# Making the second layer's linear weights in the last batch of the first layer, with the low-rank products on three quarters of the rows

## The chip, the cores and the metric

The kernel runs on one core of a Trainium2 chip. The metric is the device time of one execution in microseconds. Before the change it is 1170.06 us, the median of three runs (1169.66 to 1171.59).

## What is computed

Two transformer layers over x of shape 8 x 512 x 128, each an attention and a feed-forward block side by side on the same normalised input. The first layer has sixteen causal heads and a mixture of 32 experts of which six are taken for each row, with a shared expert. The second has four heads over two key heads, and three blocks of two linear maps each, with their weights in four bits and a low-rank addition:

```
w = q / 7.5 - 1.0                       # 6 matrices of 128 x 128
w = w * repeat(scale, 16, axis=1)
base = einsum('btd,od->bto', x, w) + bias
lora = einsum('btr,or->bto', einsum('btd,rd->btr', x, la), lb)     # r = 32
h = y + h after each block of two, with layernorm and gelu between them
```

The kernel never forms the low-rank term by rows of x. It makes one weight for each of the six maps, `w + (lb la)` transposed, before the second layer begins: the product of the two factors is a matmul over 32 rows of each.

## The kernel before, in words

The work is written out by hand for each engine, with semaphores between the engines. The first layer goes over eight batches of 512 rows. Each batch has two stages on TensorE. First come eight slots, one for each pair of heads: scores, exponentials on ScalarE, transposes of the probabilities, and the weighing of the values, whose result ScalarE copies (L859). Then come seventeen units of the experts (`units`, unit 0 is the shared one). For unit u TensorE does `project_unit(b, u)` (six matmuls of 512 columns), and from unit 3 on `unit_down(b, u - 3)` (three matmuls). Between the two, ScalarE takes the silu (L879), VectorE multiplies by the other half (`gate`, L1293) and by the routing weight of each row (`hidden`, L1303), ScalarE rounds to the high part (L869), and VectorE or POOL makes the low part (L1297, L592). The last units of a batch come down at the head of the next batch (`first_head`), before its slots; its accumulator is copied by ScalarE (L873) in slot 0. In units 5 to 15 of all but the last batch TensorE also does the rows, the router, the queries and keys and the values of the next batch. In batch 7, the last, there is no next batch; units 8, 10 and 12 carry transposes of rows of the second layer (`turn_rows`, into banks 4, 5 and 6) instead.

SP issues the DMAs in one order. In each batch it stores the routing weights (L490), loads them spread over 64 partitions, twice for each unit, into a ring of three buffers `crow` (`spread_weights`, L498, three units ahead), stores the sums of the softmax (L503), and loads these spread for each pair into `rrow` (`spread_sums0`, L510, in units 2, 3, 4, 8, 9, 10, 12, 13). A load into a ring waits until the buffer is free.

The weights of the linear maps are made in batch 0. SP loads the factors `la` and `lb` after pair 0's sums (L528, two DMAs, at unit 2). After unit 16's projection TensorE makes the six products over 32 rows into banks 4 and 5 (`add_lora`, L1550), and ScalarE copies them to `lin` (L776, L777). At the end of batch 0 SP issues ten loads (L533: the four-bit weights and scales into `crow`, the biases into `rrow`) and waits for `lin_ready`. POOL converts them (L620 to L629) and adds them to `lin` (L631) while batch 1 begins. All is needed first by `lin_in` (L1914, L1916), at the end of batch 7.

Of the kernel before, what the change touches and what calls it, by code (L numbers as in the profile page):

```python
# [14 lines left out]
P = 128  # L15
# [8 lines left out]
R, GROUP, NLIN = 32, 16, 6  # L24
BLOCKS = NLIN // 2
# [56 lines left out]
def build(nc, a, out_dram):  # L82
    with ExitStack() as ctx:
# [17 lines left out]
        wqkv_rest = sb("wqkv_rest", [P, 2 * 3 * PAIRS * P - 2 * TILES * TILES * P])  # L101
        with ExitStack() as raw:
            down_raw = raw.enter_context(nc.sbuf_tensor("down_raw", [P, UNITS, D], F32))
# [14 lines left out]
        lin = sb("lin", [P, NLIN, D])  # L118
# [86 lines left out]
        la, lb = (flat_pt[0:R, k * NLIN * D:(k + 1) * NLIN * D].rearrange("p (n d) -> p n d", n=NLIN) for k in (0, 1))  # L205
        lora = lin[:, :, :].rearrange("p i o -> p (i o)")
# [106 lines left out]
        lora_taken = sem("lora_taken")  # L313
# [136 lines left out]
        LORA_AFTER = 16  # L450
# [14 lines left out]
        lora_loads = [(la, a["la"]), (lb, a["lb"])]  # L465
# [5 lines left out]
        def _(sp):  # L471
# [40 lines left out]
            for b in range(B):  # L512
# [6 lines left out]
                for u in range(2, UNITS):  # L519
                    if u + CROWS < UNITS:  # L520
                        spread_weights(b, u + CROWS)
                    if u in SUMS_AFTER:
                        spread_sums0(b, SUMS_AFTER.index(u))
                    if b == 0:
                        sp.wait_ge(y_done, PAIRS)
                        if u == 2:
                            for dst, src in lora_loads:
                                sp.dma_start(dst, src).then_inc(lora_loaded, 16)  # L528
                if b == 0:
                    sp.wait_ge(hm_ready, UNITS - 1)  # L530
                    sp.wait_ge(y_divided, PAIRS)
                    for dst, src in w1_loads:
                        sp.dma_start(dst, src).then_inc(w1_loaded, 16)  # L533
                    sp.wait_ge(lin_ready, 1)
# [10 lines left out]
        def _(pool):  # L545
# [78 lines left out]
            def second_layer_weights():  # L624
# [4 lines left out]
                setup.step(pool.tensor_tensor(wf, wf, qs, ALU.mult))  # L629
                pool.wait_ge(lora_taken, 2)  # L630
                pool.tensor_tensor(lin[:, :, :], lin[:, :, :], wf, ALU.add).then_inc(lin_ready, 1)  # L631
# [24 lines left out]
            for b in range(B):  # L656
# [3 lines left out]
                if b == 0:  # L660
                    second_layer_weights()
                elif b < B - 1:
                    inv_sqrt1(b - 1)
# [80 lines left out]
        def _(act):  # L744
# [26 lines left out]
            def second_layer_weights():  # L771
# [3 lines left out]
                act.wait_ge(lora_done, 1)  # L775
                act.activation(lora[:, 0:512], bank[4], ACT.Copy).then_inc(lora_taken, 1)  # L776
                act.activation(lora[:, 512:NLIN * D], bank[5][:, 0:NLIN * D - 512], ACT.Copy).then_inc(lora_taken, 1)  # L777
# [107 lines left out]
            def first_layer(b):  # L885
                if b:
                    router_exps(b)
                if b == 1:
                    act.activation(temp1[:, 1:2], temp1[:, 0:1], ACT.Exp).then_inc(act_setup, 1)
                    act.wait_ge(lora_taken, 2)  # L890
# [33 lines left out]
                for u in range(UNITS):  # L924
# [12 lines left out]
                    if b < B - 1:  # L937
# [7 lines left out]
                        if b == 0 and u == LORA_AFTER:  # L945
# [152 lines left out]
        def _(dve):  # L1098
# [210 lines left out]

            def first_layer(b):  # L1310
# [22 lines left out]
                for u in range(UNITS):  # L1333
# [15 lines left out]
                    if b < B - 1:  # L1349
                        if u == ROWS_AFTER:  # L1350
                            split_xt(b + 1)
                        if u == LOGITS_AFTER:
                            take_logits(b + 1)
                low_part(b * UNITS + UNITS - 1, UNITS - 1)
# [174 lines left out]
        def _(pe):  # L1529
# [16 lines left out]
            def add_lora():  # L1546
                pe.wait_ge(lora_loaded, 16 * len(lora_loads))
                o = psum[:, 4:6, :].rearrange("p b n -> p (b n)")
                for i in range(NLIN):
                    last = mm(o[:, i * D:(i + 1) * D], la[:, i, :], lb[:, i, :], start=True, stop=True)  # L1550
# [270 lines left out]
            def first_head(b):  # L1821
# [9 lines left out]
                if b == 1:  # L1831
                    pe.wait_ge(lora_taken, 2)
# [8 lines left out]
            def units(b):  # L1841
# [12 lines left out]
                for u in range(2, UNITS):  # L1854
                    project_unit(b, u)
                    if b < B - 1:
# [10 lines left out]
                        if b == 0 and u == LORA_AFTER:  # L1867
                            pe.wait_ge(v_taken, 2 * FILLS)
                            add_lora()
                    elif u in TURN1_AFTER:  # L1870
                        g = TURN1_AFTER.index(u)
                        if g == 1:
                            pe.wait_ge(rinv0_copied, B)
                        if g == 2:
                            pe.wait_ge(y_ready, ROUNDS0)
# [428 lines left out]
```

## Time and profile before

The profiled execution took 1168.83 us, and its span from the first to the last instruction is 1167.0 us.

| | before |
|---|---|
| median of the runs | 1170.06 us |
| the profiled execution | 1168.83 us |
| its span | 1167.0 us |
| TensorE busy | 99% |
| VectorE busy | 85% |
| ScalarE busy | 70% |
| POOL busy | 35% |

Busy time is what the profile shows for each engine; TensorE's matmuls overlap, so its share says that it always has work, not that the array is full. A timeline row is the start in us, the duration, the engine, the line of the code, the operation, its tiles, the shapes and the count of instructions that were merged; in brackets stands the idle time before it and what ended that. PE is TensorE's matmuls, PEld its weight loads, DVE is VectorE, ACT ScalarE, SPq the queue of SP's DMA issues.

### The profile page before, as it was taken

How to read it: one execution, taken by the hardware profiler on the slowest of the kernel's cores; microseconds unless marked ns; L12 is line 12 of the kernel's file. 1: busy time of each engine (PE TensorE's matmuls, PEld its weight loads, DVE VectorE, ACT ScalarE, POOL GpSimd, SP SyncE). 2: the span in 40 equal slices, each digit the busy share in tenths (PEclk: the TensorE clock that was granted, in tenths of full speed). 3: DMA queues.
4: the chain of work that ended last, by engine and by line, in shares of the span. 5: the costliest groups of instructions: out<-in, count | busy, mean ns of one | idle time of the engine just before them, and what ended most of it. 6: DMA issues, size and time to landing. Idle time of an engine off the chain costs nothing.

```text
span 1167.0 us, 23979 instructions
## 1 busy us (share of the span) xinstructions
PE 1150.2 (99%) x8932; PEld 889.8 (76%) x8932; DVE 986.9 (85%) x1918; ACT 811.7 (70%) x2184; POOL 408.1 (35%) x365
## 2 busy tenths in 40 slices
PE   8999999999999999999999999999999999999998
PEld 6778778777776877677777777777778767777776
DVE  7988698979887989788888988898888778898897
ACT  6885677567756775677557765776577767877886
POOL 2326610730064006400550055005500577735741
PEclk9999999999999999999999999999999999999999
DMA  8014300410131003100320032003300330000001
GB/s 267 2 31 145 94 1 31 136 55 2 31 128 64 1 25 131 66 2 20 112 90 2 11 115 97 1 6 117 99 2 3 124 96 1 1 20 19 1 11 29
DMA packets 44565, 63.93 MB, mean 55 GB/s; under 512 B 8160, under 2 KB 18656, under 8 KB 44192
## 3 DMA queue, kind: packets, MB, share of 16 engines
q1 hardware_dynamic: 44448, 62.39, 16.6%
q8 instruction: 71, 1.16, 0.4%
q14 instruction: 46, 0.38, 0.1%
HBM read 59.48 MB, written 2.88 MB: 53 GB/s over the span
## 4 chain that ended last, share of the span: by engine, by line
PE 87%; DVE 6%; ACT 2%; issue 2%; POOL 1%; DMA 1%; SPq 0%; DVEq 0%; ACTq 0%; POOLq 0%
PE psum L1647 15%; PE psum L1666 13%; PE psum L1588 11%; PE psum L64 10%; PE psum L66 10%; PE psum L65 10%; PE psum L1703 5%; PE psum L1601 2%; PE psum L1613 2%; PE psum L1916 2%; PE psum L1670 1%; PE psum L1535 1%; PE psum L1972 1%; ACT probs L835 1%; DVE mneg L1247 1%
## 5 line engine op out<-in xcount | busy, mean ns | idle before, releaser
L793 ACT ACTIVATE probs<-psum,mneg 128x256 f32<-128x256 f32 (+3 forms) x400 | 187.3, 486 | 112.2 <-DVE mneg L1228 111.9
L1647 PE MATMUL psum<-ident,probs 128*128 128x128 f32 x1600 | 210.3, 276 | 3.6 <-ACT probs L835 3.4
L1228 DVE TENSOR_REDUCE mneg<-psum 128x2 f32<-128x1024 f32 (+3 forms) x256 | 194.1, 819 | 15.3 <-PE psum L1601 11.3
L1647 PEld LDWEIGHTS psum<-ident,probs 128*128 128x128 f32 x1600 | 178.0, 141 | 30.6 <-ACT probs L793 8.2
L1219 DVE COPY pt<-psum 128x512 f32<-128x512 f32 x256 | 164.9, 683 | 38.7 <-PE psum L1647 36.9
L592 POOL TENSOR_TENSOR qk_lo<-sg,qk_hi 128x512 fp32r<-128x512 f32 x64 | 91.7, 1438 | 155.5 <-ACT qk_hi L869 155.5
L1666 PE MATMUL psum<-pt,v_all 128*64 128x384 f32 (+5 forms) x1088 | 142.6, 412 | 0.0
L556 POOL TENSOR_TENSOR rstd<-var,mhalf 128x4 f32<-128x4 f32 x7 | 7.1, 1012 | 385.6 <-DVE var L1112 385.6
L1666 PEld LDWEIGHTS psum<-pt,v_all 128*64 128x64 f32 (+1 forms) x1088 | 69.7, 135 | 62.7 <-issue 50.2
L64 PE MATMUL psum<-xt_hi,gu_hi 128*128 128x512 f32 x272 | 110.2, 405 | 0.0
L66 PE MATMUL psum<-xt_hi,gu_lo 128*128 128x512 f32 x272 | 107.7, 396 | 0.0
L588 POOL TENSOR_TENSOR yt<-yt,rrow 128x512 f32<-128x512 f32 x64 | 98.9, 1551 | 24.5 <-DMA rrow<-sums 24.4
L65 PE MATMUL psum<-xt_lo,gu_hi 128*128 128x512 f32 x272 | 107.3, 394 | 0.0
L1303 DVE TENSOR_TENSOR sg<-sg,crow 128x512 f32<-128x512 f32 x88 | 98.3, 1117 | 7.8 <-DMA crow<-weights 5.0
L879 ACT ACTIVATE sg<-psum 128x512 f32<-128x512 f32 x96 | 57.0, 595 | 48.7 <-PE psum L66 48.6
L1588 PE MATMUL psum<-qk_hi 64*128 64x256 f32 (+3 forms) x512 | 88.5, 342 | 0.2 <-DVE v_all L1288 0.2
L1208 DVE SCALAR_TENSOR_TENSOR qk_lo<-psum,qk_hi 128x512 fp32r<-128x512 f32 x72 | 49.7, 690 | 44.5 <-ACT qk_hi L816 44.4
L793 ACT ACTIVATION_READ_ACCUMULATOR probs<-psum,mneg 128x1 f32 x400 | 83.6, 209 | 0.0
L1588 PE MATMUL psum<-qk_hi,qk_lo 64*128 64x256 f32 (+3 forms) x512 | 82.3, 318 | 0.0
L1588 PE MATMUL psum<-qk_lo,qk_hi 64*128 64x256 f32 (+3 forms) x512 | 82.3, 318 | 0.0
L869 ACT ACTIVATE qk_hi<-sg 128x512 fp32r<-128x512 f32 x96 | 60.3, 628 | 28.3 <-DVE sg L1303 28.1
L1293 DVE TENSOR_TENSOR sg<-sg,psum 128x512 f32<-128x512 f32 x96 | 65.2, 680 | 17.3 <-ACT sg L879 17.0
(294 smaller groups left out, 2762.3 us busy)
## 6 DMA issues: line engine op xcount, KB each, us to landing
crow<-weights SPq DMA_DIRECT2D x256, 128.0 KB, 2.9
rrow<-sums SPq DMA_DIRECT2D x128, 128.0 KB, 3.0
gu_raw<-in_gu SPq DMA_DIRECT2D x1, 2176.0 KB, 12.4
x_all<-in_x SPq DMA_DIRECT2D x8, 256.0 KB, 5.5
out_rows<-x_all SPq DMA_DIRECT2D x7, 256.0 KB, 2.3
down_raw<-in_down SPq DMA_DIRECT2D x1, 1088.0 KB, 13.0
wqkv_raw<-in_wqkv SPq DMA_DIRECT2D x1, 768.0 KB, 6.1
wqkv_raw<-in_wqkv SPq DMA_DIRECT2D x1, 512.0 KB, 5.1
```

What stands on the lines that cost most here:

```text
L64: nc.tensor.matmul(out, lh, rh, start=start, stop=False, **kw)
L65: nc.tensor.matmul(out, lh, rl, start=False, stop=False, **kw)
L66: return nc.tensor.matmul(out, ll, rh, start=False, stop=stop, **kw)
L588: pool.tensor_tensor(yt[:, p, :], yt[:, p, :], rrow[:, n % RROWS, :], ALU.mult).then_inc(y_divided, 1)
L592: pool.tensor_tensor(hm_lo[u % 3], sg[u % 3], hm_hi[u % 3].bitcast(F32), ALU.subtract).then_inc(pool_lo_ready, 1)
L793: last = act.activation(probs[:, h * HALF + PROB[t]:h * HALF + PROB[t] + w], bank[score_bank(rnd, c) + h][:, o:o + w], ACT.Exp, bias=mneg[ ...
L1219: dve.tensor_copy(pt[:, s % 2, :, 3 - s // 2, :], turn_bank(rnd, s).rearrange("p (j q) -> p j q", q=P)).then_inc(pt_ready, 1)
L1228: last = dve.tensor_reduce(mneg_h[:, :, t], psum[:, b:b + 2, o:o + P * (t + 1)], AX, ALU.max, negate=True)
L1303: dve.tensor_tensor(sg[u % 3], sg[u % 3], crow[:, m % CROWS, :], ALU.mult).then_inc(hm_ready, 1)
L1588: ins = mm(bank[score_bank(rnd, c) + h][:, o:o + w], ql[r, 0, qs_], kl[r, 1, ks], start=i == 0 and n == 0 and not masked, stop=masked, **K)
L1647: last = nc.tensor.transpose(dst[:, i * P:(i + 1) * P], probs[:, v:v + P], ident[:, :])
L1666: last = mm(Y[c:c + m, first * P:T], v(k), rows_t[:, k, first:TILES, :].rearrange("p t q -> p (t q)"), start=(k == 0), stop=(k == TILES - ...
```

## The change

All of the making of the weights moves to the end of the first layer, and the low-rank products take another form.

- `lin` has no memory of its own any more. It lies where the low part of the first layer's value weights was, which are read last in batch 6, for batch 7's values.
- The base weights: SP issues the ten loads at the end of batch 6 and waits there for `wf_ready` instead of `lin_ready` at the end of batch 0. POOL converts after batch 6's units, waits that the last values are made, and writes the product with the scales straight into `lin`.
- The factors: six loads instead of two. Matrix j * 3 + k goes to the k-th quarter of 32 partitions, at place j. They are issued by SP in batch 7 at the same place as before in batch 0, after pair 0's sums.
- The products: TensorE makes them in batch 7 after unit 6's projection, with the three quarters one after the other for each j, into banks 4, 5 and 6.
- The addition: VectorE adds the products to `lin` after its part of unit 6. ScalarE's two copies and POOL's addition are gone.
- Waits: `lora_taken` is gone. The waits for `rinv0_copied` and `y_ready` go from the row transposes of units 10 and 12 to `add_lora`; the transposes of unit 8 wait for `lin_ready`.

```diff
+LORA_TILES = 3
+        lin = wqkv_rest[:, PAIRS * P:PAIRS * P + NLIN * D].rearrange("p (i o) -> p i o", o=D)
-        lin = sb("lin", [P, NLIN, D])
-        la, lb = (flat_pt[0:R, k * NLIN * D:(k + 1) * NLIN * D].rearrange("p (n d) -> p n d", n=NLIN) for k in (0, 1))
-        lora = lin[:, :, :].rearrange("p i o -> p (i o)")
+        la, lb = (pt1[0:LORA_TILES * R, 0, 0, 2 * k:2 * k + 2, :] for k in (0, 1))
-        LORA_AFTER = 16
+        LORA_AFTER, W1_AFTER = 6, 16
-        lora_loads = [(la, a["la"]), (lb, a["lb"])]
+        lora_loads = [(v[r * R:(r + 1) * R, :, :], a[n].rearrange("r (j k) d -> k r j d", k=LORA_TILES)[r, :, :, :])
+                      for v, n in ((la, "la"), (lb, "lb")) for r in range(LORA_TILES)]
...
@@ SP
-                    if b == 0:
-                        sp.wait_ge(y_done, PAIRS)
-                        if u == 2:
-                            for dst, src in lora_loads:
-                                sp.dma_start(dst, src).then_inc(lora_loaded, 16)
-                if b == 0:
-                    sp.wait_ge(hm_ready, UNITS - 1)
-                    sp.wait_ge(y_divided, PAIRS)
+                    if b == B - 1 and u == 2:
+                        sp.wait_ge(y_done, ROUNDS0)
+                        for dst, src in lora_loads:
+                            sp.dma_start(dst, src).then_inc(lora_loaded, 16)
+                if b == B - 2:
+                    sp.wait_ge(hm_ready, (B - 1) * (UNITS - 1))
+                    sp.wait_ge(y_divided, (B - 1) * PAIRS)
                     for dst, src in w1_loads:
                         sp.dma_start(dst, src).then_inc(w1_loaded, 16)
-                    sp.wait_ge(lin_ready, 1)
+                    sp.wait_ge(wf_ready, 1)
@@ POOL
-                setup.step(pool.tensor_tensor(wf, wf, qs, ALU.mult))
-                pool.wait_ge(lora_taken, 2)
-                pool.tensor_tensor(lin[:, :, :], lin[:, :, :], wf, ALU.add).then_inc(lin_ready, 1)
+                pool.wait_ge(v_done, B * FILLS)
+                pool.tensor_tensor(lin, wf, qs, ALU.mult).then_inc(wf_ready, 1)
...
-                if b == 0:
+                if 0 < b < B - 1:
+                    inv_sqrt1(b - 1)
+                if b == B - 2:
                     second_layer_weights()
-                elif b < B - 1:
-                    inv_sqrt1(b - 1)
@@ ScalarE
-                act.wait_ge(lora_done, 1)
-                act.activation(lora[:, 0:512], bank[4], ACT.Copy).then_inc(lora_taken, 1)
-                act.activation(lora[:, 512:NLIN * D], bank[5][:, 0:NLIN * D - 512], ACT.Copy).then_inc(lora_taken, 1)
...
-                    act.wait_ge(lora_taken, 2)
@@ VectorE
+            def add_lora():
+                dve.wait_ge(wf_ready, 1)
+                dve.wait_ge(lora_done, 1)
+                tiles = lin.rearrange("p (j k) d -> p k j d", k=LORA_TILES)
+                products = psum[:, 4:4 + LORA_TILES, 0:2 * D].rearrange("p k (j d) -> p k j d", d=D)
+                dve.tensor_tensor(tiles, tiles, products, ALU.add).then_inc(lin_ready, 1)
...
+                    elif u == LORA_AFTER:
+                        add_lora()
@@ TensorE
                 pe.wait_ge(lora_loaded, 16 * len(lora_loads))
-                o = psum[:, 4:6, :].rearrange("p b n -> p (b n)")
-                for i in range(NLIN):
-                    last = mm(o[:, i * D:(i + 1) * D], la[:, i, :], lb[:, i, :], start=True, stop=True)
+                pe.wait_ge(rinv0_copied, B)
+                pe.wait_ge(y_ready, ROUNDS0)
+                for j in range(NLIN // LORA_TILES):
+                    for i in range(LORA_TILES):
+                        r = slice(i * R, (i + 1) * R)
+                        last = mm(bank[4 + i][:, j * D:(j + 1) * D], la[r, j, :], lb[r, j, :], start=True, stop=True)
...
-                if b == 1:
-                    pe.wait_ge(lora_taken, 2)
...
-                        if b == 0 and u == LORA_AFTER:
-                            pe.wait_ge(v_taken, 2 * FILLS)
-                            add_lora()
+                    elif u == LORA_AFTER:
+                        add_lora()
                     elif u in TURN1_AFTER:
                         g = TURN1_AFTER.index(u)
-                        if g == 1:
-                            pe.wait_ge(rinv0_copied, B)
-                        if g == 2:
-                            pe.wait_ge(y_ready, ROUNDS0)
+                        if g == 0:
+                            pe.wait_ge(lin_ready, 1)
                         turn_rows(0, g, 4)
```

## Rows read from the trace of the kernel before

**Rows 1.** The page: busy time and share, granted clock by slices, chain by engine.

```profile
PE 1150.2 (99%) x8932; PEld 889.8 (76%) x8932; DVE 986.9 (85%) x1918; ACT 811.7 (70%) x2184; POOL 408.1 (35%) x365
PEclk9999999999999999999999999999999999999999
PE 87%; DVE 6%; ACT 2%; issue 2%; POOL 1%; DMA 1%; SPq 0%; DVEq 0%; ACTq 0%; POOLq 0%
```

**Rows 2.** Timeline of ScalarE: last Y copy of batches 0 to 2, next accumulator copy.

```profile
87.97 0.60 ACT L859 ACTIVATE yt<-psum 128x512 f32<-128x512 f32 x1 [0.73 <-PE psum L1670]
...
142.90 0.60 ACT L873 ACTIVATE rrow<-psum 128x512 f32<-128x512 f32 x1 [0.22 <-PE psum L1703]
...
207.20 0.60 ACT L859 ACTIVATE yt<-psum 128x512 f32<-128x512 f32 x1 [1.20 <-PE psum L1670]
...
260.40 0.60 ACT L873 ACTIVATE rrow<-psum 128x512 f32<-128x512 f32 x1 [0.22 <-PE psum L1703]
...
324.70 0.60 ACT L859 ACTIVATE yt<-psum 128x512 f32<-128x512 f32 x1 [1.20 <-PE psum L1670]
...
378.41 0.60 ACT L873 ACTIVATE rrow<-psum 128x512 f32<-128x512 f32 x1 [0.22 <-PE psum L1703]
```

**Rows 3.** Timeline of TensorE around the low-rank products, batch 0.

```profile
126.11 0.40 PE L66 MATMUL psum<-xt_hi,gu_lo 128*128 128x512 f32 x1
...
126.43 1.60 PE L1550 MATMUL psum<-pt 32*128 32x128 f32 x12
...
127.96 0.50 PE L64 MATMUL psum<-qk_hi,down_hi 128*128 128x512 f32 x1
```

**Rows 4.** Timeline of SP's queue: the two loads of the factors, batch 0.

```profile
95.13 0.58 SPq L528 DMA_DIRECT2D pt<-in_la  x1
95.75 0.42 SPq L528 DMA_DIRECT2D pt<-in_lb  x1
```

**Rows 5.** Timeline of SP's queue, batch 7: the store, then units 1 to 5.

```profile
902.10 0.33 SPq L490 DMA_DIRECT2D weights<-comb  x1
...
914.98 4.54 SPq L498 DMA_DIRECT2D crow<-weights  x4
919.56 1.23 SPq L510 DMA_DIRECT2D rrow<-sums  x2
920.84 1.24 SPq L498 DMA_DIRECT2D crow<-weights  x2
922.13 1.23 SPq L510 DMA_DIRECT2D rrow<-sums  x2
```

**Rows 6.** First Y copies of batches 1 and 2 on ScalarE; POOL's addition, by its line.

```profile
151.58 0.62 ACT L859 ACTIVATE yt<-psum 128x512 f32<-128x512 f32 x1
...
269.09 0.63 ACT L859 ACTIVATE yt<-psum 128x512 f32<-128x512 f32 x1
...
L631 POOL TENSOR_TENSOR lin<-lin,crow x1: 1825/1825/1825, 147.6 to 147.6; 128x768 f32<-128x768 f32 x1
```

**Rows 7.** DMA issues: engine, count, KB each, median us from issue to landing.

```profile
crow<-in_qs SPq DMA_DIRECT2D x8, 48.0 KB, 2.6
...
pt<-in_la SPq DMA_DIRECT2D x1, 96.0 KB, 2.9
```

**Rows 8.** Timeline of TensorE, batch 7: the first matmul after unit 6's projection.

```profile
923.10 0.40 PE L64 MATMUL psum<-qk_hi,down_hi 128*128 128x512 f32 x1
```

**Rows 9.** Timeline of TensorE: score products, two heads on 64 rows each.

```profile
136.21 0.39 PE L1588 MATMUL psum<-qk_lo,qk_hi 64*128 64x512 f32 x2
...
136.44 0.39 PE L1588 MATMUL psum<-qk_hi,qk_lo 64*128 64x512 f32 x2
```

**Rows 10.** Timeline of VectorE, batch 7: hidden of unit 5, gate of unit 6.

```profile
922.49 0.69 DVE L1303 TENSOR_TENSOR probs<-probs,crow 128x512 f32<-128x512 f32 x1 [0.23 <-DMA crow<-weights]
...
924.12 0.69 DVE L1293 TENSOR_TENSOR sg<-sg,psum 128x512 f32<-128x512 f32 x1 [0.94 <-ACT sg L879]
```

**Rows 11.** Timeline of TensorE, batch 7: its waits for low parts after unit 6.

```profile
935.14 0.50 PE L64 MATMUL psum<-hm_third,down_hi 128*128 128x512 f32 x1 [0.52 <-DVE hm_third L1297]
...
942.50 0.50 PE L64 MATMUL psum<-hm_third,down_hi 128*128 128x512 f32 x1 [0.36 <-POOL hm_third L592]
```

More of the change, by code:

```diff
@@ L312, in build @@
         lora_done = sem("lora_done")
-        lora_taken = sem("lora_taken")
+        wf_ready = sem("wf_ready")
         lin_ready = sem("lin_ready")
@@ L944, in first_layer @@
                             take_values(b + 1, range(2 * (u - V_AFTER), 2 * (u - V_AFTER) + 2))
-                        if b == 0 and u == LORA_AFTER:
+                        if b == 0 and u == W1_AFTER:
                             second_layer_weights()
@@ L1866, in units @@
                             project_values(b + 1, range(2 * (u - V_AFTER), 2 * (u - V_AFTER) + 2))
-                        if b == 0 and u == LORA_AFTER:
-                            pe.wait_ge(v_taken, 2 * FILLS)
-                            add_lora()
+                    elif u == LORA_AFTER:
+                        add_lora()
                     elif u in TURN1_AFTER:
                         g = TURN1_AFTER.index(u)
-                        if g == 1:
-                            pe.wait_ge(rinv0_copied, B)
-                        if g == 2:
-                            pe.wait_ge(y_ready, ROUNDS0)
+                        if g == 0:
+                            pe.wait_ge(lin_ready, 1)
                         turn_rows(0, g, 4)
```

## Prediction

> **What bounds the kernel now.** I read the page first. TensorE is busy for 99% of the span, nearly all of the chain that ended last is its matmuls, and its clock stands at the upper of the two levels (2.4 GHz) in all forty slices [rows 1]. So time is lost or won only where TensorE's own queue gets longer or shorter, or where it stands still. The second view is the timeline of ScalarE at two fixed points of each batch: the copy of the last pair's Y in the unit stage (L859) and the copy of the accumulator in the next batch (L873). From the one to the other takes 142.90 - 87.97 = 54.93 us in batch 0, 53.20 us in batch 1 and 53.71 us in batch 2 [rows 2]; the later batches repeat one or the other value. Batch 0 is thus 1.2 to 1.7 us longer than its sisters, and what it alone has is the low-rank products. The third view is the timeline of all engines in the two places that the change touches, the end of batch 0's units and units 2 to 9 of batch 7.
>
> **Out of batch 0: the products.** After unit 16's last matmul at 126.11 stand twelve passes of L1550 (two for each of six fp32 products), and `unit_down` begins at 127.96 [rows 3]. From one matmul of 512 columns to the next it is 0.23 us, so the insertion takes 127.96 - 126.11 - 0.23 = 1.62 us of a TensorE that waits for nothing else. Nothing is late behind it. The low part that `unit_down(14)` wants is made long before, and the accumulator's copy follows TensorE by 0.22 us of idle [rows 2], so it moves forward with it. ScalarE also loses its two copies of the products, which were beside TensorE's work: nothing. SP loses two issues at 95.13 and 95.75 [rows 4], but TensorE doesn't stand still in these units: nothing. Gain: 1.62 us; the distance between batches bounds it at 1.2 and 1.7.
>
> **From batch 0 to batch 6: the base weights.** Ten issues on SP, SP's wait for `wf_ready`, and POOL's conversion move from the start of batch 1's attention to that of batch 7's. SP's next task there is to store the routing weights, at 902.10 in batch 7 [rows 5], some 50 us after; nothing queues behind its wait. The same POOL work lies in batch 1 now: from the accumulator's copy to the next Y copy it is 151.58 - 142.90 = 8.68 us there, and 269.09 - 260.40 = 8.69 us in batch 2 without it [rows 2, 6]. So it slows TensorE's slots not at all, and I take nothing for it in batch 7 either. POOL loses the addition of 1.83 us [rows 6], off the path. Its new wait, for the value projections of batch 7, is met before it is reached, since those are made in batch 6's units 12 to 15.
>
> **Into batch 7: six loads on SP.** They stand after unit 5's weights and pair 0's sums, that is behind 919.56 + 1.23 = 920.79, where SP now goes straight on to unit 6's weights at 920.84 and pair 1's sums at 922.13 [rows 5]. SP has no free time in this stretch. An issue of 96 KB over 32 partitions took 0.58 us behind a 64-row one and 0.42 behind its own kind [rows 4]; two issues of 64 rows take 1.23 us, 0.62 each [rows 5]. The new ones have 32 partitions with two pieces of 512 bytes each and 32 KB; no row shows this form. Bounds: 0.62 + 5 x 0.47 = 2.97 us for all, and 6 x 0.64 = 3.8 us. I take 3.1, near the 32-partition row. The last issue then starts at about 923.5 (923.3 to 924.1). From issue to landing the 96 KB loads took 2.9 us, the 48 KB ones 2.6 [rows 7]; for 32 KB I take 2.7, with 2.2 to 3.1 as bounds (2.2 is 0.4 below the median of the 48 KB loads). So the factors are there at 926.2 (925.5 to 927.2).
>
> The Trainium skill speaks against this cut: "DMA: Bandwidth & Descriptors", section "Measured (HBM→SBUF, 128 partitions, SWDGE, issued from GpSimd)", says that transfers under 64 KB are ruled by their descriptors and wants loads batched. The rows agree that half the bytes hardly save time [rows 7]. The page's fixed cost of about 2.0 us (section "Anatomy of one DMA — SWDGE (gpsimd) path") would give, as an estimate, a landing some 0.6 us sooner and a sum smaller by that; the rows of this kernel are longer, and I go by them.
>
> **Into batch 7: TensorE waits for them.** `add_lora` stands after unit 6's projection, in front of `unit_down(3)`, which starts at 923.10 today [rows 8]. TensorE's queue is in order, so it stands from 923.10 to 926.2: 3.1 us (2.4 to 4.1). Behind it wait `unit_down(3)`, unit 7's projection and all that hangs on that. Its two other new waits (`rinv0_copied`, `y_ready`) are met: SP's own issues at 914.98 come after the first, and the Y copy stands at ScalarE's unit 1.
>
> **Into batch 7: the products on row quarters.** Twelve passes again. In batch 0 they took 1.53 us one after another [rows 3]. What quarters of the rows do is not in the trace; what halves do is: two products on 64 rows each, 512 columns, begin together and the next two 0.23 us later [rows 9], the distance of one. So disjoint rows do run together. With all three quarters side by side it is 0.5 us, with none 1.6 us; the two passes of one product lie on the same rows and are next to each other in the queue, so I take half of the saving: 0.9 us.
>
> The Trainium skill, "TensorEngine Tiling (Array Packing)", section "Key Properties", says that tiles load weights and multiply in parallel, but that a change of the tiling mode drains the engine. By the first the price would be 0.5 us, by the second a little is added at either end. The halves in this trace agree with the first.
>
> **What of it is taken back.** TensorE is late by 3.1 + 0.9 = 4.0 us, the other engines only by SP's 3.1 us, because unit 6's weights land that much later: VectorE waits for its weights in unit 5 already today (0.23 us) and starts unit 6's gate at 924.12 [rows 10]. TensorE has two waits for low parts later in this stage, 0.52 and 0.36 us [rows 11]; as it arrives 0.9 us later against the others, about the first of them goes. The addition on VectorE (768 elements; 0.69 us for 512 with a PSUM operand [rows 10], so about 1.0 us) is done while TensorE does `unit_down(3)` and unit 7; it may delay gate 7 by up to 0.5 us and is what keeps the second wait alive. Batch 7: 4.0 - 0.5 = +3.5 us (2.7 to 4.5).
>
> **Sum.** -1.62 + 3.5 = +1.9 us. The profiled execution took 1168.83 us for a span of 1167.0; the change is the same on it and on the median of 1170.06, so the forecast is 1170.06 + 1.9, about 1171.9 us.
>
> **Rivals.**
> (a) Forecast, TensorE stands about 3 us for the last load: 1171.0 to 1173.2. Chance 0.60.
> (b) Slower side: SP's queue. If each new issue takes 0.62 us or more and lands after 3.1 us, the last lands at 927.2, TensorE is late by 5.0 us and the weights of units 6 and 7 by 3.8, and little is absorbed: +4.5 - 1.6 = +2.9 us, 1173.0; with 0.8 us an issue +3.9, 1174.0. It decides from 0.58 us an issue upwards. For it: pairs of 64-row issues show 0.62 [rows 5]. Against it: 0.42 at 32 partitions [rows 4]. Chance 0.17.
> (c) Slower side: the clock. The stand of 3 us is longer than any wait of TensorE in the stages around, where the clock never fell [rows 1]. If it fell, matmuls at half rate would be 0.47 instead of 0.23 us apart, 2.1 us more for each unit of nine: +4.0, 1174.0 for one unit. Chance 0.08. The Trainium skill, "TensorE: Matmul & The Clock Gate", section "HAM oscillation — how this bites in real kernels", describes such a fall after waits for a DMA. No row here shows one.
> (d) Nothing stands: the factors land before 923.10, or the later units' waits swallow the stand. Then only the products are left: -1.62 + 0.9 = -0.7, 1169.4; with both later waits gone (0.88) 1168.5. Against it: even at 0.42 us an issue the last one can't start before 923.2. Chance 0.12.
> (e) It does not do what it says: the quarters run one after another, +0.6 on (a), 1172.5; inside the range of (a).
> What is left, 0.03, is a gain of over 2.3 us by something that the trace does not show.
>
> **How the numbers follow.** 0.2% of 1170 is 2.3 us, about what a measurement of this kernel can tell from no change. Of (a), a fifth lies above 1172.4 (0.12); with nearly all of (b) and (c), 0.32 for slower. The rest of (a), (d) and a little of (b) give 0.65 for the same, and 0.03 for faster. The range goes from 1169.4 (the upper form of (d)) to 1174.2 (the upper forms of (b) and (c)).
>
> **What would show it right or wrong.** In the profile of the changed kernel: batch 0's distance between the two copies falls from 54.93 to 53.2 to 53.7 us; SP shows six issues of 0.42 to 0.6 us between 919 and 923 (all times 1.6 earlier); TensorE has one wait of about 3 us in front of L1550's matmuls, ended by a DMA; these span 0.5 to 1.6 us; batch 7's L859 to its end grows by 3 to 4 us; batch 7's first slots keep their 8.69 us. Wrong would be: no wait at L1550, a landing under 2.2 us, a lower clock after the stand, or a longer slot at the head of batch 7.

## The result, and the profile after

The changed kernel takes 1172.58 us, the median of 13 runs (1170.86 to 1173.57). The kernel before, run beside it, takes 1169.66 us (13 runs, 1167.24 to 1171.59). The ratio is 1.0026, with an interval of 1.0018 to 1.0033: about 3 us slower. The ratio is just past the bound of 0.2% that the prediction names, and the lower end of its interval just short of it. The profiled executions are 1172.82 and 1168.83 us, with spans of 1171.0 and 1167.0, so 4.0 us lie between the two that are read here.

The same two points on ScalarE as in [rows 2], now L855 and L869, first for batch 0, then for batch 7. Timeline of the changed kernel; the bracket is the idle time before and what ended it:

```profile
87.97 0.60 ACT L855 ACTIVATE yt<-psum 128x512 f32<-128x512 f32 x1 [0.73 <-PE psum L1678]
...
141.16 0.60 ACT L869 ACTIVATE rrow<-psum 128x512 f32<-128x512 f32 x1 [0.22 <-PE psum L1711]
...
911.75 0.60 ACT L855 ACTIVATE yt<-psum 128x512 f32<-128x512 f32 x1 [1.20 <-PE psum L1678]
...
965.09 0.61 ACT L869 ACTIVATE rrow<-psum 128x512 f32<-128x512 f32 x1
```

The kernel before, batch 7:

```profile
913.70 0.60 ACT L859 ACTIVATE yt<-psum 128x512 f32<-128x512 f32 x1 [1.20 <-PE psum L1670]
...
961.00 0.62 ACT L873 ACTIVATE rrow<-psum 128x512 f32<-128x512 f32 x1
```

Batch 0's distance is 141.16 - 87.97 = 53.19 us, 1.74 less than in [rows 2]. From there to the last Y copy of batch 7 another 0.2 us are scattered over the other batches, whose distances move by up to 0.5 us in either direction: 911.75 against 913.70, so 1.95 us are gained by then. Batch 7's distance goes from 47.30 to 53.34 us, **6.04 us more**. What follows, the second layer, is the same to 0.1 us. So the answer lies in batch 7 alone, and there three engines are to be read.

SP's queue in the changed kernel, where [rows 5] stood before:

```profile
918.90 1.94 SPq L528 DMA_DIRECT2D pt<-in_la  x3
920.88 1.87 SPq L528 DMA_DIRECT2D pt<-in_lb  x3
922.79 1.23 SPq L499 DMA_DIRECT2D crow<-weights  x2
```

The loads of the factors by their line, same kernel (one line for each kind: count, ns of an issue, first and last start), and their time from issue to landing:

```profile
L528 SPq DMA_DIRECT2D pt<-in_la x3: 594/595/669, 918.9 to 920.2; - x3
L528 SPq DMA_DIRECT2D pt<-in_lb x3: 593/593/594, 920.9 to 922.2; - x3
...
DMA to landing us min/median/max: 2.0/2.2/2.6
```

The six issues fill SP from 918.90 to 922.79, 3.9 us, and unit 6's weights come after them. They were the next thing in line before [rows 5].

TensorE in the changed kernel, from the end of unit 6's projection on, where [rows 8] stood:

```profile
920.91 0.40 PE L67 MATMUL psum<-xt_hi,gu_lo 128*128 128x512 f32 x1
924.32 0.79 PE L1558 MATMUL psum<-pt 32*128 32x128 f32 x12 [3.00 <-DMA pt<-in_lb]
925.04 0.80 PE L65 MATMUL psum<-qk_hi,down_hi 128*128 128x512 f32 x1
...
926.06 0.63 PE L67 MATMUL psum<-qk_hi,down_lo 128*128 128x512 f32 x1
926.49 0.63 PE L65 MATMUL psum<-xt_hi,gu_hi 128*128 128x512 f32 x1
...
928.69 0.40 PE L65 MATMUL psum<-qk_hi,down_hi 128*128 128x512 f32 x1
...
943.61 0.51 PE L65 MATMUL psum<-qk_hi,down_hi 128*128 128x512 f32 x1 [0.75 <-DVE qk_lo L1292]
...
955.23 0.50 PE L65 MATMUL psum<-qk_hi,down_hi 128*128 128x512 f32 x1 [0.63 <-DVE qk_lo L1292]
```

The clock beside it, from the table by stretches (start and end, length, then busy time and count for PE, PEld, DVE, ACT and POOL, then the granted clock as a part of the upper level, DMA share, GB/s):

```profile
922.00:924.00 2.00, 0.00 (x0) 0.00 (x0) 1.07 (x2) 1.02 (x2) 0.88 (x1) 1.00 0.19 49
924.00:926.00 2.00, 1.69 (x14) 1.36 (x15) 0.00 (x0) 0.00 (x0) 1.61 (x2) 0.71 0.57 166
926.00:928.00 2.00, 2.00 (x6) 1.55 (x5) 1.51 (x2) 0.00 (x0) 0.00 (x0) 0.50 0.62 203
928.00:930.00 2.00, 2.00 (x9) 1.59 (x9) 0.53 (x2) 1.11 (x3) 0.00 (x0) 0.94 0.63 213
```

VectorE, changed kernel:

```profile
926.49 0.69 DVE L1298 TENSOR_TENSOR sg<-sg,crow 128x512 f32<-128x512 f32 x1 [3.38 <-DMA crow<-weights]
927.10 0.95 DVE L1311 TENSOR_TENSOR wqkv_rest<-wqkv_rest,psum 128x768 f32<-128x768 f32 x1
```

Two instructions of POOL and VectorE in the same kernel, just before TensorE's wait at 943.61, and the same two in the run of "TensorE kept busy in the stand" below:

```profile
941.72 1.29 POOL L588 TENSOR_TENSOR yt<-yt,rrow 128x512 f32<-128x512 f32 x1 [0.44 <-DMA rrow<-sums]
941.75 1.80 DVE L1292 TENSOR_TENSOR qk_lo<-sg,qk_hi 128x512 fp32r<-128x512 f32 x1
```

```profile
941.02 0.68 DVE L1293 TENSOR_TENSOR qk_lo<-sg,qk_hi 128x512 fp32r<-128x512 f32 x1
941.10 1.76 POOL L589 TENSOR_TENSOR yt<-yt,rrow 128x512 f32<-128x512 f32 x1 [0.55 <-DMA rrow<-sums]
```

Taken against the last Y copy, TensorE reaches `unit_down(3)` at 13.29 us instead of 9.40, so **3.89 us late**: 924.32 - 920.91 - 0.23 = 3.18 of standing, and 0.72 for the products. The clock is still at the upper level through the stand (1.00 in the first line). It then falls to the lower one (1.2 GHz, the 0.50 in the third line), and for some three microseconds the matmuls are 0.43 us apart instead of 0.23. `unit_down(4)` begins at 16.94 instead of 11.49: **1.56 us** more. The last 0.59 us are two things. By the row transposes of unit 12 TensorE has won back 0.66 us (28.42 us behind the Y copy against 23.63, so 4.79 late instead of 5.45), mostly because the first wait of [rows 11] is gone. Then it loses 1.25 us at two waits for low parts, 0.75 and 0.63 us. The first of these low parts took VectorE 1.80 us instead of 0.68: it began 0.03 us behind an addition of POOL's, and in the other run 0.08 us ahead of it. The sum is 3.89 + 1.56 + 0.59 = 6.04. Meanwhile VectorE too is late: it stands 3.38 us for unit 6's weights.

### The profile page after: what moved, and what is told of

Same layout as the page of the kernel before. It is cut to its first block, busy times and chain, and to the rows that moved or that the text cites. A ratio compares the mean times of both kernels' runs of the same rounds, so it can differ in the third digit from the quotient of the medians.

```text
span 1171.0 us, 23968 instructions
## 1 busy us (share of the span) xinstructions
PE 1150.5 (98%) x8932; PEld 890.2 (76%) x8932; DVE 991.9 (85%) x1919; ACT 810.3 (69%) x2182; POOL 403.1 (34%) x364
## 4 chain that ended last, share of the span: by engine, by line
PE 84%; DVE 9%; ACT 3%; issue 2%; DMA 1%; SPq 1%; POOL 0%; DVEq 0%; ACTq 0%; POOLq 0%
PE psum L1655 14%; PE psum L1674 13%; PE psum L1596 11%; PE psum L65 10%; PE psum L67 9%; PE psum L66 9%; PE psum L1711 5%; PE psum L1609 2%; PE psum L1621 2%; PE psum L1919 2%; DVE probs L1298 1%; PE psum L1678 1%; DVE sg L1298 1%; PE psum L1540 1%; PE psum L1975 1%
## 5 line engine op out<-in xcount | busy, mean ns | idle before, releaser
L1298 DVE TENSOR_TENSOR sg<-sg,crow 128x512 f32<-128x512 f32 x88 | 102.8, 1168 | 9.1 <-DMA crow<-weights 6.3
```

Of the source, the lines that this page charges most:

```text
L1298: dve.tensor_tensor(sg[u % 3], sg[u % 3], crow[:, m % CROWS, :], ALU.mult).then_inc(hm_ready, 1)
```

## The experiments

From this one profile two explanations fit. Either TensorE's stand and the clock that falls after it are the loss, and VectorE's wait is covered by it; or SP's 3.9 us in front of every later weight load is the loss, and TensorE would have had to wait for VectorE anyhow. Each expectation says what the two give. The measure that is used throughout is batch 7's distance, from the last Y copy to the accumulator's copy: 47.30 us before, 53.34 after. It is read from one execution of each version. In the middle batches, where nothing was changed, this distance moves between 53.19 and 53.79 us, so differences of half a microsecond say nothing.

### The loads where SP has nothing to do

Between the weights of the first three units and the store of the sums SP issues nothing for some seven microseconds. The six loads go there, each still of 32 KB:

```diff
+                if b == B - 1:
+                    sp.wait_ge(y_done, ROUNDS0 - 4)
+                    for dst, src in lora_loads:
+                        sp.dma_start(dst, src).then_inc(lora_loaded, 16)
                 store_sums(b)
...
-                    if b == B - 1 and u == 2:
-                        sp.wait_ge(y_done, ROUNDS0)
-                        for dst, src in lora_loads:
-                            sp.dma_start(dst, src).then_inc(lora_loaded, 16)
```

> The changed kernel with its six loads of the factors moved forward on SP, from behind unit 5's weights to in front of the store of the softmax sums, where SP stands idle for about 6 us. Theory A (TensorE stands because the loads are issued late, and the fall of the clock and SP's delay follow from that): no wait of TensorE in front of the products, clock 1.000 in every execution, unit 6's weights as early as in the kernel before; batch 7 grows only by the products, 0.7 us, against 1.7 us saved in batch 0: about 1.0 us under the kernel before (ratio 0.9991). Theory B (the cost lies in the products, in VectorE's addition or in the moved base weights): the time stays near the changed kernel's, 3 us above before (ratio 1.0026).

It takes 1166.98 us (11 runs) against 1169.4 for the kernel before (27 runs): ratio 0.9984, interval 0.9975 to 0.9993. It is 1.9 us faster than the kernel before and about 5 us faster than the changed one. SP's queue, then TensorE and ScalarE, in this version:

```profile
906.29 2.59 SPq L520 DMA_DIRECT2D pt<-in_la  x3
908.93 1.87 SPq L520 DMA_DIRECT2D pt<-in_lb  x3
913.35 0.49 SPq L504 DMA_DIRECT2D sums<-rl  x1
```

```profile
922.06 0.72 PE L1558 MATMUL psum<-pt 32*128 32x128 f32 x12
...
941.53 0.50 PE L65 MATMUL psum<-hm_third,down_hi 128*128 128x512 f32 x1 [0.46 <-POOL hm_third L592]
```

```profile
912.57 0.60 ACT L855 ACTIVATE yt<-psum 128x512 f32<-128x512 f32 x1 [1.20 <-PE psum L1678]
...
960.00 0.61 ACT L869 ACTIVATE rrow<-psum 128x512 f32<-128x512 f32 x1
```

The last load is issued before 911, and SP still stands until the store at 913.35. The products have no bracket any more: nothing is waited for. Batch 7's distance is 47.43 us, 0.13 more than before; the 0.72 us of the products are nearly all taken back, most of it since the first of the two later waits of [rows 11] is gone. So the whole loss in batch 7 comes from where the loads were issued. This run doesn't say through which of the two ways, since it removes both. The clock isn't at 1.000 in every execution, as was expected, but below it in 2 of 11.

### TensorE kept busy in the stand

Fourteen products of the identity are put in front of the wait, into bank 4, which the real products overwrite:

```diff
+                pe.wait_ge(rinv0_copied, B)
+                for _ in range(KEEP):
+                    mm(bank[4][:, 0:P], ident[:, :], ident[:, :], start=True, stop=True)
                 pe.wait_ge(lora_loaded, 16 * len(lora_loads))
```

> The changed kernel, with 14 products of the identity with itself on TensorE in front of its wait for the factors (their results are overwritten). TensorE works instead of standing; the loads land no sooner. Theory A (the clock falls because TensorE stands, and that costs 1.5 us of its own): clock 1.000 in all executions, the distance from unit 6's projection to unit 3's down stays at about 3.9 us, and the time is 1.4 us under the changed kernel, +1.5 us against before (ratio 1.0013). Theory B (the slower matmuls behind the stand cost nothing, since other engines are late there anyway): the same time as the changed kernel, ratio 1.0026.

It takes 1171.0 us (11 runs), ratio 1.0016 (1.0007 to 1.0025). TensorE and ScalarE:

```profile
925.10 0.72 PE L1562 MATMUL psum<-pt 32*128 32x128 f32 x12
...
944.61 0.50 PE L66 MATMUL psum<-hm_third,down_hi 128*128 128x512 f32 x1 [0.39 <-POOL hm_third L593]
```

```profile
912.50 0.60 ACT L856 ACTIVATE yt<-psum 128x512 f32<-128x512 f32 x1 [1.20 <-PE psum L1682]
...
963.11 0.61 ACT L870 ACTIVATE rrow<-psum 128x512 f32<-128x512 f32 x1
```

The products come as late as in the changed kernel (12.60 us behind the Y copy against 12.57), so SP's part and the length of the gap are untouched; the clock is at the upper level in 9 of 11 executions. Batch 7's distance is 50.61 us, 2.73 under the changed kernel's, and by the ratios (1.0026 and 1.0016) the two differ by about 1.2 us. Of the 2.73 us, 1.48 are there by the transposes of unit 8 (19.04 and 17.56 us behind the Y copy). The other 1.25 us are the long low part and the waits behind it, which this run doesn't have. They are not the clock's: the run with two loads below has both waits (0.73 and 0.49 us) in an execution whose clock never fell in this stage. So the fall of the clock is worth 1.2 to 1.6 us, and with it healed 50.61 - 47.30 = 3.3 us of loss are left.

### The products one unit later

```diff
-        LORA_AFTER, W1_AFTER = 6, 16
+        LORA_AFTER, W1_AFTER = 7, 16
```

> The changed kernel with the products after unit 7's projection instead of unit 6's, 2.1 us of work later. SP's six issues stay where they are. Theory A (the stand is the whole of the cost): the stand shrinks from 3.2 to about 1.1 us, the clock stays up, and the time is 3.5 us under the changed kernel's: -0.6 us against before (ratio 0.9995). Theory B (SP's delay of unit 6's and 7's weights by 3.9 us costs as much by itself, through the gates and low parts that come late): the time is only 1 to 2 us under the changed kernel's, ratio 1.0010 to 1.0018, with waits of TensorE for low parts in units 9 to 12.

It takes 1175.13 us (5 runs), ratio 1.005 (1.0037 to 1.0062): slower still. Batch 7's distance is 967.62 - 913.29 = 54.33 us. TensorE, and under it VectorE:

```profile
925.80 0.72 PE L1558 MATMUL psum<-pt 32*128 32x128 f32 x12 [0.86 <-DMA pt<-in_lb]
...
932.43 0.66 PE L1540 MATMUL psum<-ident,v_all 128*128 128x128 f32 x4 [3.62 <-DVE wqkv_rest L1311]
```

```profile
928.02 0.69 DVE L1298 TENSOR_TENSOR sg<-sg,crow 128x512 f32<-128x512 f32 x1 [3.35 <-DMA crow<-weights]
930.82 0.69 DVE L1298 TENSOR_TENSOR sg<-sg,crow 128x512 f32<-128x512 f32 x1 [1.50 <-DMA crow<-weights]
931.43 0.95 DVE L1311 TENSOR_TENSOR wqkv_rest<-wqkv_rest,psum 128x768 f32<-128x768 f32 x1
```

The stand for the factors shrinks from 3.18 to 0.86 us, as it should. But unit 8's transposes wait for the addition (`lin_ready`), the addition stands behind two products with routing weights on VectorE, and these wait for late loads, 3.35 and 1.50 us. TensorE stands 3.62 us there instead, and the clock falls after that (0.50 from 934 to 936, and below 1 as a mean in all 5 executions). The stand was moved, not removed.

To take that coupling out, the addition was put in front of VectorE's routing product, all else as in the last one:

```diff
+                    if b == B - 1 and u == LORA_AFTER:
+                        add_lora()
                     if u:
...
-                    elif u == LORA_AFTER:
-                        add_lora()
```

> The changed kernel with the products after unit 7, and VectorE's addition in front of its hidden part of unit 7 instead of behind it. In the run with the addition behind, it waited for unit 7's late weights, and TensorE stood 3.6 us for the sum in front of the transposes of unit 8. Theory A (that order was the whole of the surprise): the 3.6 us are gone, the stand for the factors stays at 0.9, the clock stays up, distance in batch 7 48.5 to 50 us instead of 54.3, ratio about 0.9995 to 1.0005. Theory B (SP's delay costs by itself): 51 us or more with waits of TensorE for low parts, ratio 1.0015.

It takes 1171.51 us (11 runs), ratio 1.0013 (1.0004 to 1.0022). TensorE:

```profile
924.33 0.72 PE L1558 MATMUL psum<-pt 32*128 32x128 f32 x12 [0.81 <-DMA pt<-in_lb]
...
928.82 0.66 PE L1540 MATMUL psum<-ident,v_all 128*128 128x128 f32 x4 [1.47 <-DVE wqkv_rest L1311]
...
938.90 0.50 PE L65 MATMUL psum<-xt_hi,gu_hi 128*128 128x512 f32 x1 [0.92 <-DVE sg L1288]
```

No stand is over 1.5 us and the clock stays up in 8 of 11 executions, the profiled one among them, yet batch 7's distance is 52.40 us. The single large wait has become a row of small ones (1.47, 0.82, 0.92 and 0.48 us; two are not shown), the last ended by POOL and the others by VectorE. By the ratios half of the changed kernel's loss is gone, 1.5 of 3.0 us.

### SP's delay alone, and the stand alone

Both start from the version with the early loads. In the first the same six loads are issued a second time at their old place, into memory that nothing reads:

```diff
-                        for dst, src in lora_loads:
-                            sp.dma_start(dst, src).then_inc(lora_loaded, 16)
+                        for dst, src in again_loads:
+                            sp.dma_start(dst, src).then_inc(again_loaded, 16)
...
```

> The kernel with the factors loaded early, and in the changed kernel's place behind pair 0's sums the same six loads once more, into memory that nobody reads. SP is thus late by 3.9 us as in the changed kernel, but TensorE finds its factors and doesn't stand. Distance in batch 7 from the last Y copy to the accumulator copy: 47.4 us with the loads early, 53.3 in the changed kernel. Theory A (TensorE's stand is the cost, SP's delay is taken up by the three units between a projection and its down): 47.5 to 49 us, ratio about 0.999. Theory B (SP's delay of unit 6's and 7's weights is enough by itself: hidden, high and low part come 3 to 4 us late, and TensorE then waits in unit 9 instead): 50 to 51.5 us, ratio about 1.0010.

In the second SP is left alone and TensorE waits ahead of the products for unit 6's `hidden`, which has nothing to do with them:

```diff
                 pe.wait_ge(lora_loaded, 16 * len(lora_loads))
+                pe.wait_ge(hm_ready, (B - 1) * (UNITS - 1) + LORA_AFTER)
```

> The kernel with the factors loaded early, but TensorE waits in front of the products until VectorE has made unit 6's hidden part. TensorE stands for about 3 us at the same place as in the changed kernel, and SP is not late. Theory A (the stand and the clock are the cost): distance in batch 7 47.4 + 3.1 + 1.5, some 52 us, clock 0.997 to 0.998 in most executions, ratio 1.0022. Theory B (a stand is taken up if SP's weights are on time): 49 us or less, ratio 0.9995.

SP's delay alone: 1170.95 us (11 runs), ratio 1.0010 (1.0001 to 1.0019). Batch 7's distance is 51.41 us, 3.98 over the 47.43 of the early loads. Its TensorE (the bracket is the largest of its four waits, the others are 0.25, 0.63 and 0.48 us):

```profile
919.66 0.72 PE L1565 MATMUL psum<-pt 32*128 32x128 f32 x12
...
926.53 0.66 PE L1547 MATMUL psum<-ident,v_all 128*128 128x128 f32 x4 [1.75 <-DVE wqkv_rest L1318]
```

and its VectorE:

```profile
924.92 0.69 DVE L1305 TENSOR_TENSOR sg<-sg,crow 128x512 f32<-128x512 f32 x1 [3.39 <-DMA crow<-weights]
```

By unit 8's transposes TensorE is 1.91 us later than with the early loads (16.36 us behind the Y copy against 14.45). That half of the 3.98 us comes by the addition, which stands on VectorE behind the late product, and by the wait for `lin_ready` that the change put in front of these transposes. How much SP's delay would cost without that coupling wasn't run.

The stand alone: 1173.34 us (8 runs), ratio 1.0029 (1.0019 to 1.004). Its distance is 964.64 - 912.15 = 52.49 us, 5.06 over the early loads, and its TensorE has one line:

```profile
925.44 0.72 PE L1559 MATMUL psum<-pt 32*128 32x128 f32 x12 [3.72 <-issue]
```

The clock is below 1 in all 8 executions. TensorE comes to the products 3.80 us later than with the early loads (13.29 us behind the Y copy against 9.49), and by unit 8's transposes it is 5.35 us late: 1.55 us are what the lower level costs. In the rest of the stage 0.3 us are won back; no later wait of TensorE is left. A stand of this length without the fall of the clock, and without SP's delay, wasn't run.

So **both explanations are right, each by itself**. The delay of SP costs 4.0 us with no stand at the products, the stand with its fall of the clock 5.1 with no delay, and both together 53.34 - 47.43 = 5.9 us, far from their sum of 9.0. The ratios, set against that of the early loads (0.9984), give 3.0 us for the delay, 5.3 for the stand and 4.9 for both; the stand made here was also 0.7 us longer than the changed kernel's. Both make the same units late by the same few microseconds, one along VectorE and one along TensorE, and the later of the two counts. The run with TensorE kept busy bears this out: it has SP's delay and products just as late, but no fall of the clock, and takes 1171.0 us, where SP's delay alone takes 1170.95. On top of either comes the clock. That is why taking away only one of them brings back half at most (unit 7 with the addition first) or nothing (unit 7).

### Two loads instead of six

The factors lie in memory by quarters, so that one DMA over 96 partitions fills all three:

```diff
-        lora_loads = [(v[r * R:(r + 1) * R, :, :], a[n].rearrange("r (j k) d -> k r j d", k=LORA_TILES)[r, :, :, :])
-                      for v, n in ((la, "la"), (lb, "lb")) for r in range(LORA_TILES)]
+        lora_loads = [(la, a["la"]), (lb, a["lb"])]
```

> The changed kernel with the factors laid out by quarters in memory, so that two loads of 96 partitions do what six of 32 did, at the same place in SP's queue. Theory A (the price is the count of issues, 0.64 us each): SP is late by 1.3 us instead of 3.9, the last load lands 2.6 us sooner, TensorE stands for about 0.6 us, the clock stays up; -0.3 us against before (ratio 0.9997). Theory B (the price is the number of pieces or the bytes, not the issues): the two issues take 1.9 us each, and nothing changes against the changed kernel (ratio 1.0026).

It takes 1169.69 us (11 runs), ratio 1.0004 (0.9994 to 1.0013). SP and TensorE:

```profile
919.27 0.58 SPq L527 DMA_DIRECT2D pt<-in_la  x1
919.89 0.43 SPq L527 DMA_DIRECT2D pt<-in_lb  x1
920.37 1.09 SPq L498 DMA_DIRECT2D crow<-weights  x2
```

```profile
923.08 0.72 PE L1557 MATMUL psum<-pt 32*128 32x128 f32 x12 [1.39 <-DMA pt<-in_lb]
```

SP's delay is 1.1 us instead of 3.9, for the same bytes. The stand is 1.4 us, more than was expected, because the larger load takes about 3 us from its issue where the small ones took 2.2. The clock is below 1 in 5 of 11 executions. This is the measured price of the cut into six: 2.6 us by the ratios (1.0026 and 1.0004 of 1170 us), and 3.2 by batch 7's distances (53.34 and 50.14). It lies in the number of issues: the bytes are the same, and an issue of 96 KB in 96 pieces took no longer (0.43 to 0.58 us) than one of 32 KB in 64 pieces (0.59 to 0.67). The fall of the clock is part of this price, as the profiled execution with two loads has none behind its stand of 1.4 us.

### The base weights alone

The kernel before, with only the base weights moved to the end of batch 6:

```diff
-                if b == 0:
-                    sp.wait_ge(hm_ready, UNITS - 1)
-                    sp.wait_ge(y_divided, PAIRS)
+                if b == B - 2:
+                    sp.wait_ge(hm_ready, (B - 1) * (UNITS - 1))
+                    sp.wait_ge(y_divided, (B - 1) * PAIRS)
                     for dst, src in w1_loads:
...
```

POOL's conversion and addition, left out here, move with them.

> The kernel before with nothing but the base weights moved: SP's ten loads and its wait, and POOL's conversion with its addition, go from the end of batch 0 to the end of batch 6. The low-rank products stay in batch 0. Theory A (this part is free): ratio 1.0000 within the interval, and the head of batch 7 (accumulator copy to first Y copy) stays at 8.7 us. Theory B (POOL's or SP's work disturbs batch 7): batch 7 longer by a microsecond or more, ratio 1.001.

It takes 1169.65 us (11 runs) against 1169.72 (30 runs), ratio 1.0000 (0.9991 to 1.0008). The head of batch 7, from the accumulator's copy to the first Y copy, is 858.71 - 850.03 = 8.68 us, as everywhere (8.67 to 8.71), and the distance in batch 7 is 47.45 us. This part is free.

## Why the prediction was right or wrong

It said 1171.9 us, 1169.4 to 1174.2, with most of the chance on no difference. The time is 1172.58, inside; but the ratio is past 0.2%, on the side that was given 0.32. That the time lies near the forecast is in part luck: of the signs that the prediction itself named as showing it wrong, a lower clock after the stand came true, and the shortest landings (2.0 us) were under its 2.2. Point by point:

- **Products out of batch 0.** Said -1.62 with 1.7 as the upper bound; the distance fell by 1.74, a hair more. Right. That nothing was late behind them holds: the idle time of 0.22 us in front of the accumulator's copy is the same.
- **Base weights.** Said free; the run of that part alone shows 1.0000, and batch 7's head is unchanged. Right.
- **SP's six issues.** Said 3.1 us in all (2.97 to 3.8), from the row of 0.42; they took 3.9, at 0.59 to 0.67 each, past the upper end. This term was mis-sized. Reading the row of the second load in [rows 4] as the price of its kind was the error: in the run with two loads it is 0.43 again, where each partition's data lie in one piece as in [rows 4]. Three loads of strided pieces are nearer to the 64-row ones of [rows 5]; that the pieces are the reason isn't shown.
- **Landing.** Said 2.7 us (2.2 to 3.1); the median is 2.2. The page of the Trainium skill that was weighed there, "DMA: Bandwidth & Descriptors", section "Anatomy of one DMA — SWDGE (gpsimd) path", gives its fixed part of about 2.0 us for DMAs that GpSimd issues. These are SP's, and it was still nearer to them (2.0 to 2.6) than the rows of larger loads. Slower issues and a quicker landing cancelled out in the stand: 3.1 said, 3.18 by the starts.
- **Products on quarters.** Said 0.9 (0.5 to 1.6); 0.72 in every version, against 1.53 for the same twelve passes in [rows 3]. With 0.5 for all three side by side, that is four fifths of the saving and not the half. The rule of the Trainium skill, "TensorEngine Tiling (Array Packing)", section "Key Properties", that tiles multiply in parallel, agrees with 0.72; of its drain at a change of mode these rows show at most the 0.2 us over the estimate of 0.5.
- **TensorE late.** Said 4.0 us; 3.89 at `unit_down(3)`. Right, with the two errors above cancelling.
- **The clock, rival (c).** Said 0.08, because no stretch of the kernel before had a lower level, and left out of the sum; the granted clock is below 1 in 12 of 13 executions, and the one at 1.000 is the fastest of them all (1170.86 us). This is the step that failed. "No row here shows one" was no evidence, for no row had a stand of 3 us either: the largest in the stage was 0.52 [rows 11]. And [rows 1] could hardly have shown such a fall, as a slice there is 29 us long: the changed kernel's page has a 9 in all forty slices too. The price was less than the rival's 2.1 us a unit: 1.56, since the clock rose again after some three microseconds. The Trainium skill, "TensorE: Matmul & The Clock Gate", section "HAM oscillation — how this bites in real kernels", describes just this, a wait for a DMA and then work at the lower level. The trace agrees, but for the start: the products right behind the stand still took their 0.72 us. It deserved more than 0.08.
- **What is taken back.** Said 0.5 us, as TensorE would arrive later than the others. By unit 12's transposes it was 0.66 us here, and 0.68 to 0.80 in the runs with the early loads, with TensorE kept busy, with the stand alone and with two loads. So the reasoning held. What the sum didn't have are the 1.25 us that were lost behind it, when a low part on VectorE took 1.80 us in place of 0.68; the run with two loads lost 1.19 us in the same way, the other three nothing. In the kernel before, the timeline has 36 low parts of VectorE (L1297) in rows by themselves: 11 take 1.77 or 1.78 us and all begin while POOL adds `yt` and `rrow`, and 25 take 0.68 us and none of them does. Whether the two meet here hangs on tenths of a microsecond, so this part of the result is luck too. It is read from the traces; no run was made to test it. The wait of 0.75 us ends with that low part, while the second one, 0.63 us, is put down to it only because the same two runs have both. SP's delay of 3.9 us doesn't decide it: the run with TensorE kept busy has that delay and doesn't lose them.
- **Rival (b), SP's queue.** It decided from 0.58 us an issue, and the issues were 0.59 to 0.67. Its landing of 3.1 us didn't occur, so not its 5.0 us either. But the delay of the later weights by 3.8 us did, and by the experiment with the delay alone that is worth 4.0 us. In the sum that did no harm, since it lies beside the stand and not behind it: with the clock healed batch 7 loses 3.3 us where 3.5 were said. But counting the delay only as something which lessens the take-back hid that a cure of the stand would bring little.

So the forecast's sum was short by 2.1 us against the profile (+4.0 for +1.9): 1.56 for the clock, 1.1 for the long low part less what was taken back, less 0.1 by the gain of batch 0, 0.1 by TensorE's smaller delay, and 0.3 that scattered over the stages between and behind. Against the medians it is short by 1 us.

What stays open: why single executions of every version, the kernel before among them (5 of 27 and 8 of 30), show a granted clock of 0.997 to 0.999. The profiled execution of the base weights alone is one (0.998, 1170.96 us), and its fall lies far from all that was changed, in the second layer:

```profile
1008.91 0.63 PE L1647 MATMUL psum<-ident,probs 128*128 128x128 f32 x4 [0.82 <-ACT probs L835]
```

```profile
1012.00:1014.00 2.00, 2.00 (x12) 2.00 (x11) 1.52 (x4) 2.00 (x7) 2.00 (x4) 0.50 0.00 0
```

TensorE takes 5.33 us there from its transposes at 1010.24 to its masks at 1015.57, and 3.95 in the kernel before, where the clock stays up behind the same waits of 0.82 and 0.24 us. So such a fall costs 1.4 us, and no row says what sets it off. Open is too why the distances of the middle batches move by 0.5 us.

## What to carry to other kernels

A DMA that is added to a full queue makes everything behind it in that queue late by its issue time. Here that is 0.4 to 0.7 us for each load, whether it moves 32 or 96 KB. Look for the place where the queue already waits, and issue there: here that turns a loss of 0.26% into a gain of 0.16%. If two engines are made late by the same step, curing one shows half of it or nothing; delay each alone to see its price. And a new stand of TensorE of about three microseconds should be priced with the lower clock after it, even where the kernel before never fell, since it had no such stand.

## What the runs showed that was not expected

- After a stand of 3.0 us by the bracket the granted clock fell in 12 of 13 executions, after one of 3.7 in 8 of 8, after one of 3.6 in 5 of 5. With a longest one of 1.4 it is below 1 in 5 of 11, with one of 1.5 in 3 of 11, with one of 1.75 in 1 of 11, with none over 0.5 in 2 of 11, and in the kernel before in 8 of 30. Only for the first three does a trace show the fall right behind the stand. It cost 1.56 us there in the changed kernel and 1.55 with the stand alone.
- In the kernel before a low part on VectorE (128 x 512) took 0.68 us, and 1.78 whenever it began while POOL was adding two tiles of the same size. In the last batch of the changed kernel such a low part, with the waits behind it, cost TensorE 1.25 us.
- Fourteen small products of the identity in the gap keep the clock up and cost nothing: the real products began as late as without them.
- The same 192 KB take 1.0 us of SP's queue as two loads and 3.8 us as six, while a load of 32 KB lands after 2.2 us and one of 96 KB after about 3.0.
